# Moving layer 1's low parts and a pair of scales ahead of a layer 0 low part in GpSimd's order, in a two-layer cross-attention kernel

## The reference

```
# layer 0: 16 heads of 64
q = x @ Wq + bq ; k = ctx @ Wk + bk ; v = ctx @ Wv + bv
attn = (q k^T) * mask ; attn = exp(attn - max(attn)) * mask
attn = attn / (sum(attn) + 1e-15)
y = layernorm(attn v @ Wo + bo + x) * gamma + beta
# layer 1: 16 heads of 32
q = y @ Wq1.T ; k = ctx @ Wk1.T ; v = ctx @ Wv1.T
attn = softmax(q k^T / sqrt(32))
out = layernorm(y + (attn v) @ Wo1.T + bo1) * gamma1 + beta1
```

## Time and profile before

| what | value |
|---|---|
| time, median of 3 runs | 851.07 us (849.96 to 851.61) |
| profiled execution, own time | 850.99 us |
| its span in the trace | 849.2 us |
| granted TensorE clock over the span | 0.995 of full speed |
| TensorE busy | 829.6 us, 98% of the span |
| VectorE busy | 569.9 us, 67% |
| GpSimd busy | 448.8 us, 53% |
| ScalarE busy | 403.1 us, 47% |

### The profile page before, as it was taken

How to read it: one execution, slowest core, us unless ns; L and a number is a source line. 1 busy time by engine, 2 the same in 40 slices (tenths; PEclk the granted TensorE clock), 3 DMA queues, 4 the chain that set the end, 5 groups by cost and what they waited for, 6 DMA issues and landing times.

```text
span 849.2 us, 12709 instructions
## 1 busy us (share of the span) xinstructions
PE 829.6 (98%) x4652; PEld 561.8 (66%) x4652; DVE 569.9 (67%) x1307; ACT 403.1 (47%) x535; POOL 448.8 (53%) x285
## 2 busy tenths in 40 slices
PE   9999999999999999898999999999999999999996
PEld 6777475665657484385667577677676775776744
DVE  3567766767667585876766766747657567667587
ACT  4416373645546454733543634444536436354262
POOL 2022403123040405235878789689687886894446
PEclk9999999999999999998999999999999999999999
DMA  9518525161625044887360531433424515311002
GB/s 309 204 46 297 191 101 214 50 223 54 251 64 200 29 186 177 226 314 191 96 170 26 167 107 51 149 99 98 151 75 112 162 37 163 100 50 51 1 26 74
DMA packets 50429, 112.37 MB, mean 132 GB/s; under 512 B 4544, under 2 KB 10944, under 8 KB 50368
## 3 DMA queue, kind: packets, MB, share of 16 engines
q1 hardware_dynamic: 49408, 111.23, 40.3%
q10 hardware_dynamic: 960, 0.34, 0.2%
HBM read 77.47 MB, written 34.08 MB: 131 GB/s over the span
## 4 chain that ended last, share of the span: by engine, by line
PE 68%; POOL 12%; DVE 8%; issue 5%; DMA 3%; ACT 3%; SPq 1%; DVEq 0%; POOLq 0%; ACTq 0%
PE bank L501 15%; PE bank L502 15%; PE bank L503 14%; PE bank L557 7%; PE bank L533 6%; POOL a_raw L1585 4%; POOL a_lo L1590 4%; PE bank L540 3%; POOL a_lo L1596 3%; PE bank L695 3%; DVE scores L1304 2%; DMA r_bc<-r_dram 2%; ACT a_hi L968 1%; DMA wk_sb<-wk 1%; PE bank L667 1%
## 5 line engine op out<-in xcount | busy, mean ns | idle before, releaser
L1548 POOL TENSOR_TENSOR x_lo<-x_raw,x_hi 128x2048 fp32r<-128x2048 f32 (+1 forms) x8 | 35.6, 4448 | 196.3 <-ACT x_hi L873 180.7
L501 PE MATMUL bank<-wo_lo,a_hi 128*128 128x512 f32 x320 | 127.7, 399 | 0.0
L502 PE MATMUL bank<-wo_hi,a_lo 128*128 128x512 f32 x320 | 124.8, 390 | 0.0
L503 PE MATMUL bank<-wo_hi,a_hi 128*128 128x512 f32 x320 | 124.7, 390 | 0.0
L1159 DVE CUSTOM_DVE_ANT_0 scores<-bank,mask_f 128x512 f32<-128x512 f32 x128 | 80.8, 687 | 51.9 <-PE bank L533 51.9
L1590 POOL TENSOR_TENSOR a_lo<-a_raw,a_hi 128x1024 fp32r<-128x1024 f32 x32 | 77.4, 2421 | 50.9 <-ACT a_hi L968 50.9
L501 PE MATMUL bank<-x_lo,wq_hi 128*128 128x512 f32 x256 | 101.1, 395 | 0.5 <-DVE q_lo L1148 0.5
L988 ACT ACTIVATE scores<-scores,sh 128x512 f32<-128x512 f32 x128 | 80.3, 710 | 41.0 <-DVE sh L1329 41.0
L502 PE MATMUL bank<-x_hi,wq_lo 128*128 128x512 f32 x256 | 99.7, 390 | 0.0
L503 PE MATMUL bank<-x_hi,wq_hi 128*128 128x512 f32 x256 | 99.7, 389 | 0.0
L885 ACT ACTIVATE q_hi<-bank,bq_sb 128x512 fp32r<-128x512 f32 x64 | 44.1, 690 | 100.9 <-PE bank L503 97.3
(11 more groups left out here) (179 smaller groups left out, 1668.1 us busy)
## 6 DMA issues: line engine op xcount, KB each, us to landing
u_dram<-u_out SPq DMA_DIRECT2D x8, 2048.0 KB, 7.3
a_raw<-u_dram SPq DMA_DIRECT2D x32, 512.0 KB, 3.7
r_bc<-r_dram SPq DMA_DIRECT2D x56, 256.0 KB, 5.0
x_raw<-x_t SPq DMA_DIRECT2D x8, 1024.0 KB, 5.6
xn<-x_n SPq DMA_DIRECT2D x8, 1024.0 KB, 5.3
xb_dram<-xn SPq DMA_DIRECT2D x8, 1024.0 KB, 5.8
z<-xb_dram SPq DMA_DIRECT2D x32, 256.0 KB, 2.9
out<-z SPq DMA_DIRECT2D x6, 1024.0 KB, 7.3
```

The costliest lines, as they stand in the source:

```text
L501: nc.tensor.matmul(dst, lh, rl, start=first, stop=False)
L502: nc.tensor.matmul(dst, ll, rh, start=False, stop=False)
L503: return nc.tensor.matmul(dst, lh, rh, start=False, stop=last)
```

## The change

For blocks 1 to 6, GpSimd makes layer 1's four low parts and the scales of tiles 2 and 3 ahead of the low part of layer 0's second tile; that low part comes after the scales and ahead of `attention0(i + 1, 2)`. ScalarE makes layer 1's high parts ahead of `a0_high(i + 1, 1)`. Blocks 0 and 7 keep their order. No instruction is added or taken away.

```
@@ ScalarE @@
                 if before:
                     if more:
                         a0_high(i + 1, 0)
+                    for c in range(C1):
+                        a1_high(i - 1, c)
                     if more:
                         a0_high(i + 1, 1)
-                    for c in range(C1):
-                        a1_high(i - 1, c)
@@ GpSimd @@
                 if more:
-                    for n in (0, 1):
-                        attention0(i + 1, n)
-                        a0_low(i + 1, n)
+                    attention0(i + 1, 0)
+                    a0_low(i + 1, 0)
+                    attention0(i + 1, 1)
+                    if not before:
+                        a0_low(i + 1, 1)
                 if before:
                     for c in range(C1):
                         a1_low(i - 1, c)
                     scales0(i, 1)
+                    if more:
+                        a0_low(i + 1, 1)
```

## The result

The changed kernel takes 854.73 us in the median of 8 runs (852.28 to 856.90), the kernel before 851.04 (849.86 to 852.66). The ratio is 1.0038, with a 95% interval of 1.0022 to 1.0054: slower by 1.9 to 4.6 us, where 853.9 us was predicted. The profiled execution took 856.57 us with a span of 854.8.

What follows compares the result with a forecast made beforehand. TensorE, busy for 98% of the span, was taken as the bound. 5 x 0.55 + 0.08 = +2.8 us on the profiled 850.99 gave 853.8, or 853.9 by the median of 851.07; range 852.3 to 856.4.

Steps and rivals of the forecast that it cites:

- The removed wait: Line 764's matmuls, blocks 1 to 6: TensorE's stall for GpSimd's `a1_low` goes, 0.57 us a block, 1.03 in block 1.
- The moved scales and the low part: GpSimd, after `mv0` of tile 3: scales done 1.53 us later, low part 2.36 more, so `attention0(i + 1, 2)` 0.55 us later.
- The scales beside VectorE's `yt_low`: GpSimd's `scales0` running beside the first two `yt_low`: nothing added, since `yt_low` has one operand in PSUM, one in SBUF.
- Net in the loop: Per block: the stall of 0.57 us goes, one of about 1.12 us comes before `queries1`, net +0.55 us.
- Block 1's +0.08: In block 1, `mv0`'s end at 442.12 plus 1.53 and 2.36 gives 446.01 against 445.93: +0.08 us.
- The faster rival: `queries1` is not held and the stalls go: 3.9 us faster, 847.2 us; chance 0.05.
- the second edge: Start of `queries1`: TensorE free at 625.01, `yt_low` ends at 625.00, so making TensorE alone earlier wins nothing.
- Nothing later gives the 0.55 us back.: After `queries1`: TensorE sets the time between blocks throughout, so each block's 0.55 us loss stays to the end.
- the rival in which the new idle time costs clock: Slower by more: moved operations get longer or idle time costs clock; one us more in six blocks, 859.9; chance 0.05.
- The upper end of the range: Longest `a0_low`, 2.72 us, in all six blocks: +5.0 us in sum, plus half a us for scatter, written as 856.4.

Runs made afterwards that it cites:

- the repeat: The changed kernel, nothing altered, timed once more against the kernel before on another run of measurements: 855.28 us, ratio 1.0055 (1.0042 to 1.0068).

## Why the prediction was right, and where it was not

**The removed wait.** Right in kind: line 764 no longer waits. I priced it at 0.57 us a block; the experiments give 57.71 - 57.10 = 0.61.

**The moved scales and the low part.** Right to the hundredths: 1.53 and 2.36 us were forecast from `mv0` to the attention, 1.52 and 2.36 measured, and the attention is 0.54 us later where I said 0.55. The scales beside VectorE's `yt_low` took 620.45 - 619.09 = 1.36 us. Those of tiles 0 and 1 in the kernel before, with VectorE idle, took 601.37 - 600.00 = 1.37:

```profile
600.00 0.19 POOL L1604 TENSOR_SCALAR vs<-mv 128x2 f32<-128x2 f32 x1 [5.40 <-DVE mv L1288]
```

By the Trainium skill ("SBUF — State Buffer", section "Who interferes with whom"), a VectorE instruction with at most one SBUF input does not contend with GpSimd outside the two-port modes. The trace agrees, with 1.36 us beside `yt_low` against 1.37.

**Net in the loop.** +0.55 us a block was forecast, 58.44 - 57.91 = 0.53 measured. Block 1's +0.08 came as 9.26 - 9.16 = 0.10 from `mv0` to `queries1`.

**The faster rival.** I gave it 3.9 us and the condition that `yt_low` follows TensorE. Four kernels in which `yt_low` follows TensorE gain more, 57.91 - 57.10 = 0.81 us a block. The term that was too small is the second edge: I wrote that the two arrive within 0.04 us and left it at nothing. It costs 57.91 - 57.71 = 0.20 us a block. Of this, 0.04 us is the wait and 0.11 us is the distance from the first product to the next: 0.34 us (625.05 to 625.39) in the profile of before, 0.23 in the kernels in which `queries1` doesn't wait. The last 0.05 us was not traced.

**"Nothing later gives the 0.55 us back."** True, but something later took more. I gave 0.05 to the rival in which the new idle time costs clock, and argued against it from one longer stall without a fall. It came in both profiles, in block 7's end, at 1.4 us: 2.6 in the loop, 0.1 in block 1 and 1.4 are 4.1 us, against a measured 3.7 (1.9 to 4.6) and 4.3 (3.6 to 5.8). The sum had this term at zero. The fit isn't a proof of it: the median execution of the repeat, 855.28 us, is the one with a mean clock of 0.999, so it holds no such fall, and the scatter of the first part is larger than the term. How much the fall adds to the median stays open. What the runs show is the mechanism of the slowdown, and 2.7 us of it, 2.6 in the loop and 0.1 in block 1, against the 2.8 forecast.

**The number and the range.** 853.9 us was forecast, 854.73 and 855.28 measured, inside the range. With 2.8 us as the whole loss the repeat's interval, from 3.6 us on, would be missed, so it is partly luck that the first timing, 854.73, came so near to 853.9. The upper end of the range should read 856.5 by its own terms (850.99 + 5.0 + 0.5), where I wrote 856.4; nothing hangs on it.

## What to carry to other kernels

In an in-order queue an operation that is moved up brings its wait along: ask when its input is ready, not only who wants its output. A wait in front of an idle engine costs nothing by itself; follow what is queued behind it, through every other engine's order, to the next place where the busiest engine arrives with no margin. Where two edges meet within some hundredths of a microsecond, a gain on one side is worth nothing until the other is moved too: here one move more turned a loss of about 4 us into a gain of 4 to 6.

## What the runs showed of the hardware

A stall of 1.2 us of TensorE in block 6 went with a fall of the granted clock to 1.2 GHz for 3.5 us some 75 us later, behind a stretch in which TensorE was busy for 5.53 of 5.80 us; the same stretch without the stall in block 6 kept 2.4 GHz. That the stall makes it was tried by placing it (blocks 1 to 5 without a fall, block 6 alone with one); each placing was seen in one profile. Two executions of kernels with that stall had mean clocks of 0.999 and 1.000, in which no such fall can be, so it does not come each time, and how the stall reaches that far stays open.

A product of `queries1` that waits costs more than its wait: the distance to the next product is then 0.34 us in place of 0.23, with a wait of 0.04 us as with one of 1.19.
